# One MoE layer over four batches: y tiles stored as they lie and gathered when combined, a third PSUM bank for the first layer, the second layer three tiles behind

## The reference

```python
adj = emb_s * emb_t
att = jax.nn.softmax(attention_weights, axis=-1) * (1.0 / np.sqrt(n).astype(np.float32))
adj = adj * att
adj = adj.at[:, diag, diag].set(-jnp.inf)
_, idx = jax.lax.top_k(flat, k)
out = jnp.zeros((g, n * n), dtype=adj.dtype).at[rows, idx].set(1.0)
...
scores = jax.nn.softmax(jnp.einsum('bsh,he->bse', x, G), axis=-1)
value, indices = jax.lax.top_k(scores, TOPK)
w = jnp.einsum('bsk,bske->bse', value, onehot)
gate = jax.nn.silu(jnp.einsum('bsh,efh->bsef', x, gate_w))
up = jnp.einsum('bsh,efh->bsef', x, up_w)
out = jnp.einsum('bsef,bse,ehf->bsh', gate * up, w, down_w)
lr = jnp.einsum('bsh,erh->bser', x, lora_A)
out = out + LORA_SCALE * jnp.einsum('bser,bse,ehr->bsh', lr, w, lora_B)
...
x = x + _L0_ffn_ref(_L0_cond_ref(fside, cond[:, None, :], x, 10240), G, gate_w, up_w, down_w, lora_A, lora_B)
```

## Time and profile before

| | us |
|---|---|
| three runs | 800.79 (median), 798.49, 806.63 |
| the profiled execution, whole | 801.54 |
| its span, on which all rows stand | 799.8 |
| VectorE busy | 523.6 |
| PE busy | 500.9 |
| ScalarE busy | 442.2 |
| GpSimd busy | 389.5 |

### The profile page before, as it was taken

The page is one execution under the profiler, slowest core; times in us unless marked ns, Lnnn a source line. Parts: engine busy times, 40 slices in busy tenths (PEclk is TensorE's granted clock), DMA queues, the critical chain, the costliest instruction groups (busy, mean ns, idle before and its releaser), DMA issues.

```text
span 799.8 us, 13618 instructions
## 1 busy us (share of the span) xinstructions
PE 500.9 (63%) x3682; PEld 330.4 (41%) x3682; DVE 523.6 (65%) x1242; ACT 442.2 (55%) x655; POOL 389.5 (49%) x337
## 2 busy tenths in 40 slices
PE   0211187259878882788777717977669469788800
PEld 0200076146545551455445414544436246455400
DVE  5768789857598686776786867757872723343245
ACT  6687278738845476297445653973336345455300
POOL 7114200045366123588886136768971177877400
PEclk9755599669999895799999957998988869999865
DMA  9990060013312453368368733575478238767469
GB/s 317 360 269 0 3 261 28 0 49 113 113 74 91 166 217 107 125 226 283 133 220 272 299 102 131 206 261 175 169 252 326 94 102 287 262 207 260 164 259 381
DMA packets 76984, 147.29 MB, mean 184 GB/s; under 512 B 21475, under 2 KB 30699, under 8 KB 76400
## 3 DMA queue, kind: packets, MB, share of 16 engines
q1 hardware_dynamic: 59248, 104.40, 38.4%
q0 software_dynamic: 17664, 41.98, 14.7%
HBM read 95.47 MB, written 69.21 MB: 206 GB/s over the span
## 4 chain that ended last, share of the span: by engine, by line
DVE 20%; DMA 18%; issue 15%; POOL 14%; PE 13%; ACT 8%; DVEq 7%; SPq 2%; POOLq 1%; ACTq 0%
DMA put_rows<-y,where 5%; DMA piece<-put_rows 5%; DMA out_dram<-piece 5%; PE pa L690 4%; DVE mask L1075 4%; ACT mask L805 3%; POOL piece L538 3%; POOL xg L521 3%; DVE small L1037 3%; POOL piece L541 3%; DMA w<-put_rows 2%; ACT y L862 2%; DVEq L1364 2%; DVEq L1031 1%; DVE g_parts L1365 1%
## 5 line engine op out<-in xcount | busy, mean ns | idle before, releaser
L690 PE MATMUL pa<-w,xt 128*128 x1472 | 209.2, 296 | 5.4 <-issue 4.3
L862 ACT ACTIVATE y<-pc,where 128x512 f32<-128x512 f32 x184 | 121.7, 688 | 150.8 <-DMA put_rows<-y,where 94.6
L690 PEld LDWEIGHTS pa<-w,xt 128*128 128x128 f16 x1472 | 149.2, 102 | 74.1 <-issue 25.7
L529 POOL DMA_INDIRECT put_rows<-y,where x92 | 92.1, 1001 | 134.4 <-ACT y L862 114.0
L521 POOL DMA_INDIRECT xg<-mask_rows,where x92 | 99.1, 1078 | 115.8 <-DVEq L1349 95.0
L1357 DVE SCALAR_TENSOR_TENSOR g_full<-pa,where,s_act 128x144 f32<-128x144 f32 x92 | 33.5, 364 | 177.2 <-ACT s_act L854 177.2
L849 ACT ACTIVATE xt<-pb 128x1024 f16<-128x1024 uint8 x92 | 94.2, 1024 | 46.7 <-PE pb L677 46.5
L713 PE MATMUL pc<-wd,gt 128*128 x184 | 75.6, 411 | 13.1 <-ACT y L862 11.9
L714 PE MATMUL pc<-wd,gt 128*128 x184 | 75.9, 413 | 0.0
L715 PE MATMUL pc<-wd,gt 128*128 x184 | 75.5, 410 | 0.0
L716 PE MATMUL pc<-lb,gt 128*128 x184 | 75.5, 410 | 0.0
(11 more groups left out here) (208 smaller groups left out, 864.9 us busy)
## 6 DMA issues: line engine op xcount, KB each, us to landing
piece<-put_rows SPq DMA_DIRECT2D x96, 256.0 KB, 3.9
v<-in_x_dram SPq DMA_DIRECT2D x40, 512.0 KB, 8.5
piece<-in_x_dram SPq DMA_DIRECT2D x48, 256.0 KB, 2.9
out_dram<-piece SPq DMA_DIRECT2D x48, 256.0 KB
w<-put_rows SPq DMA_DIRECT2D x16, 512.0 KB, 9.6
w<-in_L_ffn_gate_w_dram SPq DMA_DIRECT2D x8, 512.0 KB, 10.3
w<-in_L_ffn_up_w_dram SPq DMA_DIRECT2D x8, 512.0 KB, 8.3
wd<-in_L_ffn_down_w_dram SPq DMA_DIRECT2D x8, 512.0 KB, 9.5
```

The costliest lines, as they stand in the source:

```text
L529: pool.indirect_dma_start(out=put_rows[n % 2], out_offset=bass.IndirectOffsetOnAxis(ap=put_row[n][:, i:i + 1], axis=0), in_=y[:, g % NY, : ...
L690: last = pe.matmul(l1[g % 2], xt[:, g % 2, t, :], w1[:, bass.ds(e, 1), t, k, :].rearrange("p o n -> p (o n)"), start=(t == 0 and k == 0), ...
L862: nc.scalar.activation(y[:, g % NY, half * HALF:(half + 1) * HALF], pc[:, half, :], ACT.Copy, scale=y_scale[n][:, i:i + 1]).then_inc(y_rea ...
```

## The change

Four things change. (1) SP stores each y tile as it lies, padding too, by a plain DMA (`store_tile`, `y_rows`). The store of tile i-4 stands in SP's step i, behind that step's output store, x load and mask move. (2) In the next batch GpSimd gathers, for each block c of 128 tokens and each of its two experts, the 128 rows of y (**pair** k = 2c + r, `gather_pair`, 512 KB, into the one buffer `piece[:, 2]`) and adds them to the x block in the step behind (`add_pair`, 1024 columns). Pairs 0 to 8 are gathered in steps 0 to 8, pairs 9 to 15 in steps 13 to 19. The output block c is stored when pair 2c + 1 is added. The x load of the batch after next and the mask store stand at step 21. (3) The first layer has three banks; its third is `pd`, so the mask's turned parts share the bank of `xt_ps` (upper half), with waits on both sides, and at other spots. (4) The second layer runs three tiles behind, g is turned two behind, y is evicted three behind, so that at a batch's end one more tile of each is left over. In the diff below, SP's and GpSimd's new functions stand without the lines that they replace, which are in the listing above.

```diff
+    NL = 3
     NX, NY = 5, 2
 
-    PIECES, NC = 2 * C, 2
+    NC = 2
+    BACK = 4
...
-    TURN_AT = {(18, 3): 0, (19, 0): 1, (19, 3): 2, (20, 0): 3, (20, 3): 4, (21, 0): 5, (21, 3): 6, (22, 0): 7}
-    STORE_MT_AT = {(18, 3): 0, (19, 0): 1, (19, 3): 2, (20, 0): 3, (20, 3): 4, (21, 0): 5, (21, 3): 6, (22, 0): 7}
+    TURN_AT = {(18, 3): 0, (19, 3): 1, (20, 3): 2, (21, 0): 3, (21, 2): 4, (21, 3): 5, (22, 0): 6, (22, 2): 7}
+    STORE_MT_AT = {(18, 3): 0, (19, 3): 1, (20, 3): 2, (21, 0): 3, (21, 1): 4, (21, 3): 5, (22, 0): 6, (22, 1): 7}
     MAX_AT = {(19, 2): 0, (20, 0): 1, (20, 1): 2, (20, 2): 3, (21, 0): 4, (21, 2): 5, (22, 0): 6, (22, 2): 7}
 
 
-    PIECE_AT = {**{j + 1: j for j in range(9)}, **{j + 4: j for j in range(9, PIECES)}}
-    PIECES_FIRST = 14
+    PAIR_AT = {**{k: k for k in range(9)}, **{k + 4: k for k in range(9, Q)}}
+    ADD_AT = {i + 1: k for i, k in PAIR_AT.items()}
+    STORE_OUT_AT = {i + 2: k // ROLES for i, k in PAIR_AT.items() if k % ROLES}
+    LOAD_X_AT = {i + 1: c + NC for i, c in STORE_OUT_AT.items() if c + NC < C}
+    NEXT_X_AT = 21
...
-        piece = sb("piece", [P, NC, 3, HALF], F32)
+        piece = sb("piece", [P, NC + 1, H], F32)
...
-        l1 = [pa[:, i, 0:N1] for i in range(2)]
+        l1 = [pa[:, 0, 0:N1], pa[:, 1, 0:N1], pd[:, 0:N1]]
         xt_ps = words(pb[:, 0, :])
         gt_ps = blocks(pb[:, 1, :])[:, 0:3, :]
-        mt_ps = words(pd[:, :])
-        spread_ps = pd[:, 0:NEAR * P]
+        first_mt_ps, mt_ps = words(pd[:, :]), blocks(pb[:, 0, :])[:, HT // 2:HT, :]
+        spread_ps = pm[:, 0:NEAR * P]
...
-        put_rows = [nc.dram_tensor(f"put_rows{i}", [ROLES * S, H], F32, kind="Internal").ap() for i in range(2)]
+        y_rows = [nc.dram_tensor(f"y_rows{i}", [T * P, H], F32, kind="Internal").ap() for i in range(2)]
...
+            def store_tile(n, i):
+                g = tile(n, i)
+                sp.wait_ge(y_ready, 2 * (g + 1))
+                if i == 0 and n >= 2:
+                    sp.wait_ge(pair_added, Q * (n - 1))
+                sp.dma_start(y_rows[n % 2][i * P:(i + 1) * P, :], y[:, g % NY, :]).then_inc(y_stored[g % NY], 16)
+
+            def load_piece(n, c):
+                u = C * n + c
                 if u >= NC:
+                    sp.wait_ge(piece_stored[u % NC], 16 * (u // NC))
+                sp.dma_start(piece[:, u % NC, :], x_rows[n][:, c, :]).then_inc(piece_landed[u % NC], 16)
+
+            def store_piece(n, c):
+                u = C * n + c
+                sp.wait_ge(pair_added, ROLES * (u + 1))
+                sp.dma_start(out_rows[n][:, c, :], piece[:, u % NC, :]).then_inc(piece_stored[u % NC], 16)
...
+                if n == 1:
+                    sp.wait_ge(b_turned, 4)
+                    sp.wait_ge(a_turned, 1)
+                if n > 0:
+                    for c in range(NC):
+                        load_piece(n - 1, c)
+                for i in range(T):
+                    if n > 0 and i in STORE_OUT_AT:
+                        store_piece(n - 1, STORE_OUT_AT[i])
+                    if n > 0 and i in LOAD_X_AT:
+                        load_piece(n - 1, LOAD_X_AT[i])
+                    if n + 1 < B and i == NEXT_X_AT:
+                        move_mask(n + 1)
+                    if i >= BACK:
+                        store_tile(n, i - BACK)
+                for i in range(T - BACK, T):
+                    store_tile(n, i)
...
+            def wait_stored(n):
+                for i in range(NY):
+                    pool.wait_ge(y_stored[i], 16 * len(range(i, T * (n + 1), NY)))
+
+            def gather_pair(n, k):
+                u = Q * n + k
+                if u > 0:
+                    pool.wait_ge(pair_added, u)
                 pool.indirect_dma_start(
+                    out=piece[:, NC, :], out_offset=None, in_=y_rows[n % 2],
+                    in_offset=bass.IndirectOffsetOnAxis(ap=pair_slot[n][:, k:k + 1], axis=0),
+                    bounds_check=T * P - 1, oob_is_err=False).then_inc(pair_landed, 16)
+
+            def add_pair(n, k):
+                u, v_of = Q * n + k, C * n + k // ROLES
+                pool.wait_ge(pair_landed, 16 * (u + 1))
+                if k % ROLES == 0:
+                    pool.wait_ge(piece_landed[v_of % NC], 16 * (v_of // NC + 1))
+                else:
+                    pool.wait_ge(pair_added, u)
+                nc.gpsimd.tensor_tensor(piece[:, v_of % NC, :], piece[:, v_of % NC, :], piece[:, NC, :],
+                                        ALU.add).then_inc(pair_added, 1)
 
             for n in range(B):
                 pool.wait_ge(routed, n + 1)
                 pool.wait_ge(mask_stored, 16 * (n + 1))
                 for i in range(NX):
                     gather(n, i)
                 for i in range(T):
                     if i == DIAG_AT and n + 1 < B:
                         diagonal(n + 1)
                     if i + NX < T:
                         gather(n, i + NX)
+                    if n > 0 and i in ADD_AT:
+                        add_pair(n - 1, ADD_AT[i])
+                    if n > 0 and i in PAIR_AT:
+                        if PAIR_AT[i] == 0:
+                            wait_stored(n - 1)
+                        gather_pair(n - 1, PAIR_AT[i])
                     if n + 1 < B and i in BELOW_AT:
                         for q in BELOW_AT[i]:
                             below_third(n + 1, q)
+
+            n = B - 1
+            wait_stored(n)
+            for c in range(C):
+                for r in range(ROLES):
+                    pool.indirect_dma_start(
+                        out=last_put[c][r], out_offset=None, in_=y_rows[n % 2],
+                        in_offset=bass.IndirectOffsetOnAxis(ap=pair_slot[n][:, ROLES * c + r:ROLES * c + r + 1],
+                                                            axis=0),
+                        bounds_check=T * P - 1, oob_is_err=False).then_inc(rows_landed[c], 16)
...
-            def turn_mask(n, c):
+            def turn_mask(n, c, evicted=0):
                 pe.wait_ge(mask_ready, n + 1)
                 if n > 0 or c > 0:
                     pe.wait_ge(mt_ready, C * n + c)
+                if evicted:
+                    pe.wait_ge(xt_ready, evicted)
+                into = mt_ps if n > 0 else first_mt_ps
                 turned = words_of(mask_8[:, c * S:(c + 1) * S])
                 for t in range(HT // 2):
-                    last = pe.transpose(mt_ps[:, t, :], turned[:, t, :], ident[:, :])
+                    last = pe.transpose(into[:, t, :], turned[:, t, :], ident[:, :])
...
-            def turn_x(n, i):
+            def turn_x(n, i, masks=0):
                 g = tile(n, i)
+                if masks:
+                    pe.wait_ge(mt_ready, C * (n + 1) + masks)
...
-                if g >= 2:
-                    pe.wait_ge(g_ready, g - 1)
+                if g >= NL:
+                    pe.wait_ge(l1_free, g - NL + 1)
...
-                    if i >= 1:
-                        turn_g(n, i - 1)
+                    if i >= 2:
+                        turn_g(n, i - 2)
                     between(i, 2)
-                    if i >= 2:
-                        second_layer(n, i - 2, experts[i - 2])
+                    if i >= 3:
+                        second_layer(n, i - 3, experts[i - 3])
...
+                turn_g(n, T - 2)
+                second_layer(n, T - 3, experts[T - 3])
...
-                    if i >= 2:
-                        store_y(n, i - 2, 0)
+                    if i >= 3:
+                        store_y(n, i - 3, 0)
                     between(i, 2)
-                    if i >= 2:
-                        store_y(n, i - 2, 1)
+                    if i >= 3:
+                        store_y(n, i - 3, 1)
                     between(i, 3)
+                store_y(n, T - 3, 0)
+                store_y(n, T - 3, 1)
...
+                if n >= 2:
+                    dve.wait_ge(pair_added, Q * (n - 1))
+                V.tensor_copy(pair_slot[n], slot)
...
-                V.tensor_copy(put_row[n], none_here)
...
-                    if i >= 1:
-                        store_gt(n, i - 1)
+                    if i >= 2:
+                        store_gt(n, i - 2)
                     between(i, 2)
+                store_gt(n, T - 2)
```

128 lines of the change are left out of this document (35 added, 93 removed).

## The result

The changed kernel takes 960.92 us (median of 4 runs, 956.92 to 962.3) where the kernel before takes 799.64 us beside it: a ratio of 1.199, 95% interval 1.191 to 1.207. I had said 864 us, with 815 to 905 as range. The direction was right, the loss is 2.6 times as large.

The account below looks back on a forecast made before the run. The prediction took VectorE's own work for the next batch and chains between engines as the bound. Its terms 10.6 + 22.2 + 15.1 + 13.8 + 1 = 62.7 us, added to the profiled 801.5 us, gave 864 us, range 815 to 905.

Parts of the forecast that it names:

- The pairs: GpSimd's strict chain of gather and add delays batches 1, 2 and 3 by 22.2, 15.1 and 13.8 us.
- the term p: Period of one pair on GpSimd, landing plus add plus about 0.2: 6.7 us, with ends 5.8 and 8.0.
- Rival (1): Pair gathers land as fast as the x gather, 3.1 us: period 5.8 us, time 834 us; chance 0.2.
- the product 3.0 us late: In batch 1, GpSimd's first product for the next batch starts at 384.8 instead of 381.76, after pair 8.
- "Nothing" for lag and third bank: In the expert loop every index shifts and every wait stays: no gain; the longer tail is priced within the switch.
- pure order: Batch 0's switch: y(17)'s store behind x loads and mask store puts the exponential 10.6 us later.
- x loads and mask store: At the switches, standing at step 21 ahead of y(17)'s store, they put the exponential 28.8 us after the loads.
- Rival (2): At the switches y stores are not held behind x loads, only the mask store counts: 847 us; chance 0.11.
- (3): Pairs keep up with the tiles at 5.2 us or less, SP frees y buffers at once: 778 us; chance 0.12.
- (4): Pair gathers slow to 5.3 us and more beside x, y and output traffic: 918 us; chance 0.07.
- The end: After the last y, the same 8 MB read by 16 gathers, 21 us issue against 23 us transfer: +1 us.

Follow-up runs that it names:

- Experiment 3: Changed kernel with x block loads and output stores of batches 0 to 2 cut to 16 of 1024 columns: 924.2 us (one run).
- Experiment 8: Changed kernel with each pair's gather by index replaced by a plain load of 128 neighbouring rows: 898.5 us (one run).
- 5, half of the rows: Changed kernel with pairs gathered and added on 512 of 1024 columns in batches 0 to 2, y stored in two halves there: 847.6 us.
- Experiment 6: Changed kernel in which GpSimd, not SP, issues the output stores and the loads of x's blocks for the combination: 906.1 us, ratio 1.138.
- experiment 2: Changed kernel with the x loads and mask store at SP's step 18 instead of step 21: 941.0 us, ratio 1.176.
- experiments 1: Kernel before with only the third bank, the moved mask parts and the lag, keeping the old path of y: 811.8 us, ratio 1.015.
- 12: Changed kernel with gathers accumulating onto three x blocks in SBUF, but two first-layer banks and no extra lag: 823.7 us, ratio 1.027.
- experiment 7: Changed kernel with its new path of y, but two first-layer banks, second layer two tiles behind and mask parts in their own bank: 958.4 us.
- 11: Changed kernel with gathers accumulating onto x's block in SBUF, no landing buffer or GpSimd add, three x blocks: 836.3 us, ratio 1.044.
- 13: Version with accumulating gathers, two banks and no extra lag, with a block's two gathers set two steps apart: 815.9 us, ratio 1.017.

## Why the prediction was right in sign and wrong in size

**The step that failed: "The pairs", the term p.** I put p = 6.7 us from 4.0 of landing, 2.5 of add and "about 0.2". Measured: 5.84, 2.42 and 0.77, in all 9.03 of a period of 9.07. Of the miss of 2.37 us, 1.84 is the landing. I took it from the median of the put, which goes the other way, and my upper end of 5.3 (an estimate for which I gave no working) was too low as well. The rest is mostly the gap from an add to the next gather, 0.77 for 0.2. Rival (1) by the Trainium skill, "DMA: Bandwidth & Descriptors", section "Anatomy of one DMA — SWDGE (gpsimd) path", came to 3.2 us for 512 KB, an estimate; the trace disagrees: the median landing is 4.6 us, and the fastest start of an add 4.22 us after the issue. Of the 1.84 us, 0.64 are there in the gathers without a burst (4.64 for 4.0). The other 1.2 come from the 7.04 us of those beside one, for a reason that I did not draw: SP waits for the pairs, so its transfers go out in a burst with the next gather. Experiment 3 puts 0.75 us on the part of it that is x and output. Experiment 8 puts 1.4 us of the period on the index (issue, gap and landing).

**The count of pairs held, the path only in part.** From p = 8.0, the upper end, my sums of 39.1, 31.2 and 34.6 us for batches 1, 2 and 3 grow by 13, 13 and 16 us for each us of p. Carried on to 9.07 they give 53.0, 45.1 and 51.7 us; measured were 54.3, 45.4 and 51.1. This shows that nearly every pair's lateness counts once. It does not show by which queue it travels, for the lateness is the same in SP's and in GpSimd's. A series of doses shows the same without any of my formulas:

| kernel | period, us | time, us |
|---|---|---|
| changed | 9.07 | 960.9 |
| 3, less traffic | 8.28 | 924.2 |
| 8, plain loads | 7.67 | 898.5 |
| 5, half of the rows | 6.65 | 847.6 |

From the first to the last it is 113.3 us for 2.42 us of period, 47 us for each, with 48 pairs in the kernel. Each of these edits changes something beside the period (the traffic, the form of the DMA, the number of y's stores), and two of them have one run, so the slope is rough: 42 to 50 us from one row to the next. It holds for SP's order as it is. Experiment 6 has nearly the period of the first row and is at 906.1, experiment 2 (9.12 us) at 941.0. My range failed by the bound on one duration.

**SP's order and GpSimd's order.** I named SP's queue as part of the chain, with y's stores behind it. Taking the pairs out of it gives back 55 us (experiment 6). I gave GpSimd's own queue two small terms (the product 3.0 us late); with SP freed it carries the greater part of the loss alone, by PE's waits for expert rows, which my sum did not have. That the sum still came out right at 9.07 us is in part luck: whichever queue carries it, the lateness of the pairs has the same size.

**"Nothing" for lag and third bank: wrong by 10 to 13 us.** So much they cost in the kernel with the old path of y and in the one with accumulating gathers (experiments 1, 12); it is right only where the pairs hide it (7). I had followed each wait in the loop and found it unchanged; that PE's waits inside the loop stay is not what costs. Of the +5.1 us of batch 0 (I had said +10.6, "pure order"), the lag alone gives 5.7 and the new order alone 2.9 (experiment 7, 154.9 for 152.0). The exponentials show it too: 302.3 in the changed kernel and 302.7 with the lag alone, for 296.9 before. So what I called a loss by the order of SP's stores is, in batch 0, as large with the old stores.

**x loads and mask store.** In batch 2 y's stores do hold up y(19) behind them, as I said: 17.8 us where I had 20.8. Rival (2) falls with that. The exponentials of all three switches follow 26.4 to 26.5 us after the loads, near my 28.8, but in batches 0 and 1 this agreement is luck: y(19) did not wait for a store there. In batch 1 VectorE waited 33 us for x itself, in batch 0 6.3 us, a path that I had missed, and batch 0 has the longer tail besides. In batch 0 the loads went out at 275.75, not 278.7, and the exponential came 5.4 us later than before, half of my 10.6.

**Rivals (3) and (4).** (3) needed a period of 5.2 us, never reached in any version that adds on GpSimd (6.55 was the shortest), so it stays untested. Without pairs the kernel is at 782.7 us, near the 778 that I gave it, but there the adds are gone too. (4), slow landings, came nearest, and I gave it 0.07, a landing of 5.3 and 918 us.

**The end**: I said +1 us; it is 4.6 from the last y on (42.3 for 37.7).

## What to carry to other kernels

A buffer that holds one transfer at a time turns "read ahead" into "ask, land, use, signal, ask", and its period has to be compared with the pace of the loop with every gap in it; here each us of period cost some 47 us, with 48 such transfers. Bound such a landing by the slowest transfers beside which it will run and ask what the waiting queue will send in one burst when it is let go: an issue-to-landing median of another transfer is no upper bound. And look at each in-order queue in which something waits for the chain, for the issues standing behind that wait are late as well; freeing one of two such queues gave back only a third. When the sum then agrees, look whether the long wait is the one that was named: two switches here had the right length by another path.

## What the runs showed of the hardware

- On GpSimd an indirect gather that waits for GpSimd's own add starts 0.77 us after the add's end; a plain DMA in its place 0.30 us. The issue itself takes 1.01 us against 0.58, and 1.55 us where it accumulates.
- The gather of 512 KB by index has a median landing of 4.6 us, with 4.2 to 8.6 us from issue to add: 4.64 on average where SP is quiet, 7.04 where most have three or four of SP's transfers beside them. Accumulating in SBUF the median landing is 7.8 to 8.3 us (experiments 11 to 13).
- In the stage of batch 1 PE waited more, its granted clock fell from 0.88 to 0.79, and the same matmuls took 123.6 instead of 115.4 us of busy time. How much of this lengthened the stage no run shows.
